# Experts with four buffers, sums by a tree, and half of the shared expert moved behind the experts

## The chip, the core and the metric

The program runs on one core of a Trainium2 chip, as a single launch. The metric is device time in microseconds (us), the median of several executions. The engines are TensorE (PE, its weight loads PEld), VectorE (DVE), ScalarE (ACT), GpSimd (POOL) and SyncE (SP), which here only issues transfers. Each engine works through its own list of instructions in order and waits on semaphores; a transfer is issued by an engine and then runs on 16 DMA engines.

## What is computed

Two transformer layers on 4096 tokens of width 256, all in float32. Layer 0 is an attention with 16 heads and linear biases, then a mixture of 64 experts; layer 1 is a rotary causal attention of one head, then a gated linear attention.

```python
x = L0_attn_x                                         # 1 x 4096 x 256
h = _layernorm(x) * (1 + ca) + sa
x = x + ga * _L0_attn_ref(h, L0_attn_W_kqv)
h = _layernorm(x) * (1 + cb) + sb
x = x + gb * _L0_ffn_ref(h, ...)                      # routed experts + shared expert
...
x = x + ga * _L1_attn_ref(h, ...)
...
x = x + gb * _L1_ffn_ref(h, ...)

# _L0_ffn_ref: 64 experts, 8 for each token, at most 256 tokens to an expert
h = silu(einsum('ech,efh->ecf', xe, w1)) * einsum('ech,efh->ecf', xe, w3)
ye = einsum('ecf,ehf->ech', h, w2)
out = segment_sum(vals * flat_w[:, None], flat_t, num_segments=T)   # the 8 rows of each token
shared = silu(x @ shared_gate.T) * (x @ shared_up.T) @ shared_down.T
return out + shared
```

## The kernel before

The residual `xres` stays in SBUF: 32 tiles of 128 tokens, in 8 chunks of 4 tiles (512 tokens). The program is a series of blocks; each ends when all engines and all its transfers are done, and only then does the next one start. The order on each engine is written out by hand. The blocks are these, with the stretch of the profiled execution (span 5162.3 us) in which each lies:

- `project_heads` (34 to 209 us): for each chunk the norm on DVE, transposes `psT`, the four blocks `psQ` of queries and keys and the values `psV` on PE. ACT copies `psQ` to `parts[b][:, 0]` (L287), DVE puts the remainder in `parts[b][:, 1]` (L327), and SP stores both parts to `q_laid` and `k_laid` (L260): 8 transfers of 256 KB a chunk. There is one buffer `parts[b]` for each block, so ACT's copy of a chunk waits for the stores of the one before. ACT copies the values to `vbuf` (L295) and issues four stores to `v_aug` itself (L300), in pieces of 512 bytes. Behind these on ACT stands the square root (L201) for which the norm of the next chunk but one waits.
- `bias_attention` (209 to 2909 us): the attention of layer 0; at its side the tokens of seven of the eight chunks are normalised (kept in `hT_rows`), routed and scattered to `x_rows`.
- `shared_expert` (2909 to 3028 us): norm and routing of the last chunk (`last_c`, 7), then `send_rows`: 32 indirect scatters by POOL (L577), each waiting for the last but one to have landed (`two_under_way`). PE does the shared expert for all eight chunks: `gate_up` (L1421, 16 products of 512 columns), ACT `Silu` (L1342), DVE `multiply` (L1364), PE `down` (L1433), DVE `add_shared` (L1370, L1374). Chunks 0 and 1 go beside the routing; 2 to 7 come after it.
- `experts` (3028 to 3318 us): a loop over 64 experts. In iteration e PE does `turn(e+2)` (transposes `psX`, L1627), `first(e+1)` (`psH`, `psU`, L1638) and `last(e)` (`psY`, L1647). DVE's `pick` takes the weights of the tokens, `multiply` makes `hidden`, and `scale` (L1601) makes `y`. SP issues four transfers an iteration: `x` of expert e+4 (320 KB) once `turn(e+2)` and `pick(e+2)` are done, `w1w3` of e+3 (256 KB), `w2` of e+2 (128 KB) and the store of `y` (256 KB). Everything has two buffers.
- `rope_attention` (3318 to 4107 us): POOL gathers eight rows of `y_rows` for each token, 8 indirect transfers a tile (L1724), into `rows[n % 2]`. DVE's `sum_rows(n)` is a reduction over 2048 elements (L1892), a product with the gate (L1895) and a sum into `xres` (L1896). At first four tiles are summed, then come `statistics(0)`, `normalise(0)` (L1921 to L1929), PE's `turn_h(0)` (L1737), `heads` with DVE's `rotate`, and tiles 4 and 5. Then runs the loop over 32 tiles of queries, where tile s holds `sum_rows(s + 6)` ahead of `maximum(s + 1)` on DVE; ACT's exponential of tile s+1 needs that maximum (`ra_top`), and PE's transposes `psT` of tile s+1 need the exponential.
- `low_rank` and `linear_attention` (4107 to 5162 us).

```python
def sum_rows(n):
    dve.wait_ge(gathered[n % 2], 16 * TOPK * (n // 2 + 1))
    dve.tensor_reduce(total[n % 2][:, :], rows[n % 2][:, :, :].rearrange("p k d -> p d k"), AX,
                      ALU.add).then_inc(rows_read, 1)
```

## Time and profile before

| | us |
|---|---|
| median of 3 runs | 5146.05 |
| lowest, highest | 5146.01, 5150.23 |
| profiled execution | 5163.93, of which the span is 5162.3 |
| PE, DVE busy in it | 4681.8 (91%), 4057.1 (79%) |
| ACT, POOL busy in it | 3071.8 (60%), 1114.2 (22%) |

The profile is of one execution, 17.9 us longer than the median of the runs. Since every block ends with a meeting of all engines, the span is the sum of its blocks, and each block has a limit of its own. What a piece of work is worth is therefore read inside its block, by which wait there ends last, and not from the shares of the whole span.

### The profile page before, as it was taken

To read this page: it belongs to the slowest core of one execution; us is meant where nothing else is said; L and a number is where in the kernel's file an instruction comes from. 1 tells how busy PE (TensorE), PEld (TensorE's weight loads), DVE (VectorE), ACT (ScalarE), POOL (GpSimd) and SP (SyncE) were. 2 spreads that over 40 slices of the span, in tenths; PEclk is the share of its full clock that TensorE was granted. 3 is DMA by queue.
4 is the path that set the end of the run, shared out by engine and by line. 5 is a ranking of instruction groups with operands and counts; after the bars stand their busy time and mean duration, and the time that the engine had idled before them with its cause. 6 is when DMAs were issued, how large, how long until landed. Compare 5 with 4: busy or idle time off the path is not lost. (4 is left out here: it accounts for less than half of the span.)

```text
span 5162.3 us, 101254 instructions
## 1 busy us (share of the span) xinstructions
PE 4681.8 (91%) x39032; PEld 2403.0 (47%) x39032; DVE 4057.1 (79%) x5031; ACT 3071.8 (60%) x5309; POOL 1114.2 (22%) x1152
## 2 busy tenths in 40 slices
PE   5589999999999999999999888547899969999998
PEld 3233333333333333333333456425566646666666
DVE  4499999999999999999998233377765448788787
ACT  1158888888888888888888512112222225555554
POOL 0000012102121021211212210254320004444443
PEclk8679999999999999999999989879999979999999
DMA  5736545354443534444342137632110031111010
GB/s 181 165 87 156 137 75 114 67 90 90 80 81 71 89 72 89 78 75 85 67 86 53 33 107 224 202 95 79 60 55 4 11 125 31 28 27 29 25 29 17
DMA packets 242778, 421.66 MB, mean 82 GB/s; under 512 B 42569, under 2 KB 147034, under 8 KB 242256
## 3 DMA queue, kind: packets, MB, share of 16 engines
q1 hardware_dynamic: 195504, 341.87, 30.1%
q0 software_dynamic: 30048, 66.76, 4.1%
q10 hardware_dynamic: 16896, 8.39, 0.7%
q8 instruction: 236, 3.87, 0.3%
q14 instruction: 94, 0.77, 0.1%
HBM read 324.51 MB, written 129.17 MB: 88 GB/s over the span
## 5 line engine op out<-in xcount | busy, mean ns | idle before, releaser
L1100 DVE TENSOR_REDUCE attn_mpart<-attn_ps_max 128x2 f32<-128x1024 f32 x2048 | 2450.0, 1221 | 100.6 <-PE attn_ps_max L1154 95.0
L837 ACT ACTIVATE attn_probs<-attn_ps_exp 128x512 f32<-128x512 f32 x4096 | 2226.7, 595 | 315.0 <-PE attn_ps_exp L1170 231.4
L1154 PE MATMUL attn_ps_max<-attn_keys,attn_quer 54*128 54x512 f32 x4096 | 1481.4, 458 | 69.9 <-DMA attn_keys<-k_laid 37.9
L1170 PE MATMUL attn_ps_exp<-attn_quer,attn_keys 54*128 54x512 f32 x4096 | 1504.2, 447 | 0.2 <-ACT attn_probs L837 0.2
L1185 PE MATMUL attn_ps_out<-attn_probs,attn_vals 128*32 128x256 f32 x16384 | 1310.1, 391 | 9.8 <-ACT route_o L842 9.2
L1170 PEld LDWEIGHTS attn_ps_exp<-attn_quer,attn_keys 54*128 54x128 f32 x4096 | 616.2, 185 | 836.2 <-ACT attn_probs L837 781.4
L1185 PEld LDWEIGHTS attn_ps_out<-attn_probs,attn_vals 128*32 128x32 f32 x16384 | 323.4, 108 | 750.3 <-issue 394.9
L1154 PEld LDWEIGHTS attn_ps_max<-attn_keys,attn_quer 54*128 54x128 f32 x4096 | 591.7, 188 | 119.3 <-DVE attn_mpart L1100 75.9
L1724 POOL DMA_INDIRECT ra_rows<-y_rows,slots x256 | 252.8, 987 | 300.8 <-DVE ra_total L1892 227.0
L577 POOL DMA_INDIRECT x_rows<-route_pay,route_now x256 | 252.0, 984 | 299.9 <-DMA x_rows<-route_pay,route_now 213.0
L1856 ACT ACTIVATE ra_row<-ra_psS 128x512 f32<-128x512 f32 x112 | 66.9, 597 | 360.9 <-PE ra_psS L1777 360.9
L1796 PE MATMUL ra_psO<-ra_vals,ra_probT 128*128 128x256 f32 x1056 | 256.5, 388 | 7.8 <-DVE ra_probT L1972 7.8
L2379 POOL TENSOR_TENSOR gla_ke<-gla_kg,emask 128x512 f32<-128x512 f32 x128 | 152.2, 1217 | 514.7 <-DVE gla_kg L2605 514.7
L1777 PE MATMUL ra_psS<-ra_kT,ra_qT 128*128 128x512 f32 (+3 forms) x576 | 240.7, 573 | 6.6 <-DVE ra_kT L1942 6.6
L1796 PEld LDWEIGHTS ra_psO<-ra_vals,ra_probT 128*128 128x128 f32 x1056 | 198.9, 196 | 42.4 <-DVE ra_probT L1972 10.0
L2670 PE MATMUL gla_psP<-gla_wqkv,gla_hc 128*128 128x512 f32 x384 | 189.7, 631 | 2.5 <-ACT gla_egn L2459 2.0
L2464 ACT ACTIVATE gla_sq<-gla_psO 128x512 f32<-128x512 f32 x32 | 19.1, 597 | 266.4 <-PE gla_psO L2778 266.4
L2365 POOL TENSOR_TENSOR gla_qeT<-gla_ftT,gla_emr 128x512 f32<-128x512 f32 x128 | 173.1, 1385 | 14.0 <-ACT gla_ftT L2411 14.0
L1777 PEld LDWEIGHTS ra_psS<-ra_kT,ra_qT 128*128 128x128 f32 x576 | 109.2, 197 | 124.8 <-issue 114.3
L1594 DVE TENSOR_TENSOR exp_hidden<-exp_psU,exp_gate 128x256 f32<-128x256 f32 x64 | 27.2, 425 | 174.0 <-PE exp_psY L1647 144.1
L1972 DVE COPY ra_probT<-ra_psT 128x512 f32<-128x512 f32 (+2 forms) x144 | 90.2, 644 | 84.6 <-PE ra_psT L1787 83.7
L1892 DVE TENSOR_REDUCE ra_total<-ra_rows 128x256 f32<-128x2048 f32 x32 | 116.9, 3653 | 39.7 <-DMA ra_rows<-y_rows,slots 39.7
(390 smaller groups left out, 5346.8 us busy)
## 6 DMA issues: line engine op xcount, KB each, us to landing
attn_keys<-k_laid SPq DMA_DIRECT2D x256, 256.0 KB
attn_vals<-v_aug SPq DMA_DIRECT2D x128, 512.0 KB, 7.7
attn_keys<-k_laid SPq DMA_DIRECT2D x256, 128.0 KB
x_rows<-attn_zeros POOLq DMA_DIRECT2D x16, 1280.0 KB, 6.2
exp_x<-x_rows SPq DMA_DIRECT2D x64, 320.0 KB
exp_w1w<-in_w SPq DMA_DIRECT2D x64, 256.0 KB
y_rows<-exp_y SPq DMA_DIRECT2D x64, 256.0 KB
attn_keys<-k_laid SPq DMA_DIRECT2D x256, 48.0 KB
```

Of the source, the lines that this page charges most:

```text
L577: pool.indirect_dma_start(out=x_rows, out_offset=bass.IndirectOffsetOnAxis(ap=r.now[:, n, k:k + 1].bitcast(U32), axis=0), in_=r.pay[:, n, ...
L837: act.activation(probs[k % 2][:, j, :], ps_exp[bank_of(g, n)][:, :], ACT.Exp).then_inc(exp_done, 1)
L1100: dve.tensor_reduce(mpart[i][:, kb, TC * pair + tile::TC * NPR], ps_max[buffer][:, :, :], AX, ALU.max).then_inc(unit_read, 1)
L1154: mm = pe.matmul(ps_max[buffer][:, h, :], quer[at % NG][half(h), pair, tile * P:(tile + 1) * P], keys[at % 2][half(h), pair, kb * CH:(kb + ...
L1170: pe.matmul(ps_exp[bank_of(g, n)][:, :], keys[g % 2][half(h), pair, k * P:(k + 1) * P], quer[g][half(h), pair, :], start=True, stop=True). ...
L1185: mm = pe.matmul(ps_out[j * VW:(j + 1) * VW, n], vals[:, k, j * VW:(j + 1) * VW], probs[k % 2][:, j, n], start=(k == 0 and q == 0), stop=( ...
L1724: pool.indirect_dma_start(out=rows[n % 2][:, k, :], out_offset=None, in_=y_rows, in_offset=bass.IndirectOffsetOnAxis(ap=slots[:, n, k:k + ...
L1777: mm = pe.matmul(psS[g % 2][:, 0:width], qT[s // TC % 2][:, k, s % TC * P:(s % TC + 1) * P], kT[:, k, b * BLK:b * BLK + width], start=(k = ...
L1796: mm = pe.matmul(psO[s % 2][:, :], probT[(before(s) + b) % 2][:, j * P:(j + 1) * P], vals[:, n, :], start=(n == 0), stop=(n == s))
L2365: last = pool.tensor_tensor(qeT[:, b, :, :], ftT[:, 3, b, :].unsqueeze(1).to_broadcast([P, NE, P]), emr[i][:, :, :], ALU.mult)
L2379: last = pool.tensor_tensor(ke[i][:, e, :], kg2[:, :], emask[:, bass.ds(m, 1), e].to_broadcast([P, KDV]), ALU.mult)
L2670: mm = pe.matmul(ps, hc[i][:, k, :], wqkv[:, x, k, :], start=(k == 0), stop=(k == KD - 1))
```

## The change

- **Projection**: `parts` gets a second set of four buffers, so that ACT's copy of a chunk waits for the stores of the chunk before the last. `vbuf` is laid out by groups of heads, so that a store goes in pieces of 2048 bytes; POOL issues one store of 1 MB a chunk in place of ACT's four; ACT copies the values in four pieces, not two.
- **Shared expert**: `shared_expert` does chunks 0, 1, 2 and 7. Its scatters wait for the last but three. Chunks 3 to 6 go to the head of `rope_attention`, beside the gathers, with weights and activations in parts of `row` that aren't in use yet.
- **Experts**: `x`, `w1w3` and `w2` get four buffers, and SP loads `x` of e+6, `w1w3` of e+5 and `w2` of e+4. `y`, `xT`, `hidden` and all of PSUM keep two. `scale` multiplies with the gate as well.
- **Sums**: `sum_rows` adds in halves (1024, 512 and 256 elements) in place of the reduction; its product with the gate is gone.

```diff
-        parts = [sb(f"parts{b}", [P, NPART, CH], F32R) for b in range(4)]
-        vbuf = [sb(f"vbuf{i}", [P, TC, H0, VW]) for i in range(2)]
+        parts = [[sb(f"parts{i}{b}", [P, NPART, CH], F32R) for b in range(4)] for i in range(2)]
+        vbuf = [sb(f"vbuf{i}", [P, NG, TC, HG * VW]) for i in range(2)]
...
+                with pool.Fori(0, NC // 2) as t:
+                    for i in range(2):
+                        hold(pool, v_copied, NG * (2 * t + i + 1), pool_passed)
+                        pool.dma_start(v_aug[:, :, bass.ds((2 * t + i) * TC, TC), :].rearrange("g p n w -> p g n w"),
+                                       vbuf[i][:, :, :, :]).then_inc(v_stored[i], 16)
...
-                        act.wait_ge(parts_stored[b], 16 * NPART * c)
+                        act.wait_ge(parts_stored[i][b], 16 * NPART * t)
...
-                    for g in range(NG):
-                        act.dma_start(v_aug[g, :, bass.ds(c * TC, TC), :],
-                                      vbuf[i][:, :, HG * g:HG * g + HG, :].rearrange("p n h w -> p n (h w)")
-                                      ).then_inc(v_stored[i], 16)
...
+SHARED_HERE = (0, 1, 2, NC - 1)
+SHARED_LATER = (3, 4, 5, 6)
...
-                    if i >= 2:
-                        pool.wait_ge(scattered[i % 2], 16 * (i // 2))
+                    if i >= 4:
+                        pool.wait_ge(scattered[i % 4], 16 * (i // 4))
...
-                for c in range(2, NC):
-                    gate_up(c)
-                    down(c - 1)
-                down(last_c)
+                for i in range(2, len(SHARED_HERE)):
+                    gate_up(i)
+                    down(i - 1)
+                down(len(SHARED_HERE) - 1)
...
+        DEEP = 4
...
-                    if more(4):
+                    if more(DEEP + 2):
...
-                        load_x(e + 4, i)
-                    if more(3):
+                        load_x(e + DEEP + 2, (i + 2) % DEEP)
+                    if more(DEEP + 1):
                         hold(sp, h_summed, e + 2, sp_passed)
-                        load_w13(e + 3, 1 - i)
-                    if more(2):
+                        load_w13(e + DEEP + 1, (i + 1) % DEEP)
+                    if more(DEEP):
                         hold(sp, y_summed, CT * (e + 1), sp_passed)
-                        load_w2(e + 2, i)
+                        load_w2(e + DEEP, i)
...
-                        dve.tensor_scalar(y[i][:, c, :], psY[i][:, c, :], wrow[i][:, c:c + 1], None,
-                                          ALU.mult).then_inc(y_copied, 1)
+                        dve.scalar_tensor_tensor(out=y[i % 2][:, c, :], in0=psY[i % 2][:, c, :],
+                                                 scalar=wrow[i % 2][:, c:c + 1], in1=mod[:, GB, :],
+                                                 op0=ALU.mult, op1=ALU.mult).then_inc(y_copied, 1)
...
+                pe.wait_ge(sw_loaded, 48)
+                gate_up(0)
+                for i in range(1, len(SHARED_LATER)):
+                    gate_up(i)
+                    down(i - 1)
+                down(len(SHARED_LATER) - 1, range(2))
                 pe.wait_ge(w_loaded, 16)
                 turn_h(0)
+                down(len(SHARED_LATER) - 1, range(2, TC))
...
-                    dve.tensor_reduce(total[n % 2][:, :], rows[n % 2][:, :, :].rearrange("p k d -> p d k"), AX,
-                                      ALU.add).then_inc(rows_read, 1)
+                    at = rows[n % 2]
+                    summing(dve.tensor_tensor(at[:, 0:4, :], at[:, 0:4, :], at[:, 4:8, :], ALU.add))
+                    summing(dve.tensor_tensor(at[:, 0:2, :], at[:, 0:2, :], at[:, 2:4, :], ALU.add))
+                    dve.tensor_tensor(total[n % 2][:, :], at[:, 0, :], at[:, 1, :], ALU.add).then_inc(rows_read, 1)
                     dve.wait_ge(rows_read, n + 1)
-                    summing(dve.tensor_tensor(total[n % 2][:, :], total[n % 2][:, :], mod_before[:, GB, :], ALU.mult))
                     summing(dve.tensor_tensor(xres[:, n, :], xres[:, n, :], total[n % 2][:, :], ALU.add))
...
                 for n in range(TC):
+                    if n < len(SHARED_LATER):
+                        multiply(n)
                     sum_rows(n)
+                    if n + 1 < len(SHARED_LATER):
+                        add_shared(n)
                 statistics(0)
                 normalise(0)
+                add_shared(len(SHARED_LATER) - 1)
```

The new `gate_up`, `down`, `multiply` and `add_shared` in `rope_attention` are those of `shared_expert` with other buffers, except that `down` and `add_shared` go tile by tile (256 columns) through the two buffers `psO`.

On ACT, in the loop of the projection, this stood from the second copy of the values to the next square root:

```order
L294 REGISTER_ALU
L295 ACTIVATE proj_vbuf<-proj_psV 128x32x16
L298 ISA
L300 ISA
L300 DMA v_aug<-proj_vbuf 128x4x128
L300 ISA
L300 DMA v_aug<-proj_vbuf 128x4x128
```

and this stands there now, the values' copies halved in size:

```order
L306 REGISTER_ALU
L308 ACTIVATE proj_vbuf<-proj_psV 128x4x4x16 x2
L306 REGISTER_ALU
L308 ACTIVATE proj_vbuf<-proj_psV 128x4x4x16 x2
L200 ISA
L201 ACTIVATE proj_rstd<-proj_rstd 128x4
```

The square root no longer stands behind four issues; the store is now alone in a loop of POOL.

On DVE, at the head of the rotary attention, this stood for the first two of the four tiles:

```order
L1892 TENSOR_REDUCE ra_total<-ra_rows 128x256
L1895 TENSOR_TENSOR ra_total<-ra_total,mod 128x256
L1896 TENSOR_TENSOR xres<-xres,ra_total 128x256
L1892 TENSOR_REDUCE ra_total<-ra_rows 128x256
L1895 TENSOR_TENSOR ra_total<-ra_total,mod 128x256
L1896 TENSOR_TENSOR xres<-xres,ra_total 128x256
```

and this stands there now for the first one (L2090 is the shared expert's `multiply`, L2096 and L2098 its `add_shared`):

```order
L2090 TENSOR_TENSOR ra_row<-ra_psT,ra_row 128x512 x2
L1973 TENSOR_TENSOR ra_rows<-ra_rows 128x1024
L1974 TENSOR_TENSOR ra_rows<-ra_rows 128x512
L1975 TENSOR_TENSOR ra_total<-ra_rows 128x256
L1977 TENSOR_TENSOR xres<-xres,ra_total 128x256
L2096 TENSOR_TENSOR ra_row<-ra_psO,mod 128x256
L2098 TENSOR_TENSOR xres<-xres,ra_row 128x256
L2096 TENSOR_TENSOR ra_row<-ra_psO,mod 128x256
L2098 TENSOR_TENSOR xres<-xres,ra_row 128x256
```

So each of the four sums stands behind a `multiply` that waits for PE and ACT, and ahead of an `add_shared` that waits for PE.

On PE, in the same place, the shared expert's products now stand around the transposes of the first chunk, `turn_h(0)` (L1784), which used to be the first in the block:

```order
L1878 MATMUL ra_psS<-ra_row 128x512 x2
L1878 MATMUL ra_psT<-ra_row 128x512 x2
L1888 MATMUL ra_psO<-ra_row 128x256 x12
L1784 MATMUL ra_psR<-ident,ra_h_head 128x128 x8
L1888 MATMUL ra_psO<-ra_row 128x256 x4
L1793 MATMUL ra_psR<-ra_hT,ra_w 128x512
```

The last half of the fourth chunk's `down` lies between the transposes and the first of the `heads`.

## Rows read from the trace of the kernel before

**Rows 1.** Window, attention block: PE, PEld, DVE, ACT, POOL busy, clock, DMA share, GB/s

```profile
209.19:2908.90 2699.71, 2643.71 (x24870) 1000.35 (x24870) 2532.70 (x2568) 2261.05 (x4185) 431.93 (x485) 0.98 0.45 86
```

**Rows 2.** Timeline of the projection: start, duration, instruction, [idle before, releaser]

```profile
100.03 0.60 ACT L287 ACTIVATE proj_parts<-proj_psQ 128x512 fp32r<-128x512 f32 x1 [7.07 <-DMA k_laid<-proj_parts]
102.74 5.65 ACTq L300 DMA_DIRECT2D v_aug<-proj_vbuf  x4
```

**Rows 3.** The same timeline, issues by SP and the end of the block

```profile
113.94 3.46 SPq L260 DMA_DIRECT2D q_laid<-proj_parts  x4
117.64 7.67 SPq L260 DMA_DIRECT2D k_laid<-proj_parts  x4
...
190.22 6.93 SPq L260 DMA_DIRECT2D k_laid<-proj_parts  x4
209.19 2.39 SPq L718 DMA_DIRECT2D attn_quer<-q_laid  x6
```

**Rows 4.** The same timeline, PE without a wait

```profile
59.44 1.04 PE L348 MATMUL proj_psT<-ident,proj_h 128*128 128x128 f32 x8
...
63.77 7.03 PE L357 MATMUL proj_psQ<-proj_hT,proj_w_kqv 128*128 128x512 f32 x16
```

**Rows 5.** DMA queues from 46 to 200 us: packets, MB, share of 16 engines

```profile
q1 hardware_dynamic: 10625, 21.50, 42.8%
q10 hardware_dynamic: 16486, 8.19, 22.3%
```

**Rows 6.** Timeline of the scatters on POOL, and SP's first issue for the experts

```profile
2949.74 0.97 POOL L577 DMA_INDIRECT x_rows<-route_pay,route_now  x1 [0.30 <-issue]
...
2999.75 0.97 POOL L577 DMA_INDIRECT x_rows<-route_pay,route_now  x1 [0.61 <-issue]
...
3028.15 0.38 SPq L1520 DMA_DIRECT2D exp_x<-x_rows  x1
```

**Rows 7.** Timeline of PE, shared expert: two chunks

```profile
2985.03 1.96 PE L1421 MATMUL disp_psG<-disp_hs,disp_wg 128*128 128x512 f32 x4 [0.88 <-DVE disp_actT L1364]
...
2996.47 1.95 PE L1421 MATMUL disp_psG<-disp_hs,disp_wg 128*128 128x512 f32 x4 [0.88 <-DVE disp_actT L1364]
```

**Rows 8.** DMA queue from 3060 to 3290 us, in the experts

```profile
q1 hardware_dynamic: 43819, 51.85, 71.2%
```

**Rows 9.** Timeline of PE in the experts: first(1), first(2), and turn(63)

```profile
3038.97 1.03 PE L1638 MATMUL exp_psH<-exp_xT,exp_w1w 128*128 128x256 f32 x4
...
3041.99 1.03 PE L1638 MATMUL exp_psH<-exp_xT,exp_w1w 128*128 128x256 f32 x4
...
3305.96 0.66 PE L1627 MATMUL exp_psX<-ident,exp_x 128*128 128x128 f32 x4 [0.64 <-DMA exp_x<-x_rows]
```

**Rows 10.** Waits of PE from 3044 to 3315 us: total, times, longest

```profile
PE exp_psX L1627 <- DMA exp_x<-x_rows: 36.4, 45, 1.9
```

**Rows 11.** Timeline of the rotary attention's head

```profile
3361.86 3.59 DVE L1892 TENSOR_REDUCE ra_total<-ra_rows 128x256 f32<-128x2048 f32 x1 [5.59 <-DMA ra_rows<-y_rows,slots]
3365.49 0.42 DVE L1895 TENSOR_TENSOR ra_total<-ra_total,mod 128x256 f32<-128x256 f32 x1
...
3373.98 1.94 PE L1737 MATMUL ra_psR<-ident,ra_h_head 128*128 128x128 f32 x8 [60.17 <-DVE ra_h_head L1929]
...
3407.95 3.59 DVE L1892 TENSOR_REDUCE ra_total<-ra_rows 128x256 f32<-128x2048 f32 x1 [3.91 <-DMA ra_rows<-y_rows,slots]
```

**Rows 12.** Timeline of DVE and POOL around 3562 us

```profile
3562.25 1.23 DVE L1925 TENSOR_TENSOR ra_scratch<-ra_scratch,mod 128x1024 f32<-128x1024 f32 x1
...
3562.40 1.89 POOL L1724 DMA_INDIRECT ra_rows<-y_rows,slots  x1 [0.30 <-issue]
```

**Rows 13.** Waits of PE from 3457 to 3920 us

```profile
PE ra_psT L1787 <- ACT ra_row L1864: 11.8, 5, 5.1
PE ra_psR L1737 <- DVE ra_h_head L1929: 11.3, 4, 4.3
PE ra_psR L1746 <- ACT ra_hT L1840: 11.1, 4, 4.9
```

## What the change will do to the time

> **What bounds the kernel now.** I read the windows by block first, since blocks never overlap, then in each block the waits of its busiest engine, and the timeline where a wait repeats. The attention is more than half of the span and none of it is touched: PE is busy 2643.7 of its 2699.7 us [rows 1]. The change touches four places, and in each the profile shows something else that ends last.
>
> In the projection it is a ring of issues. PE without waits does a chunk in 63.77 + 7.03 - 59.44 = 11.36 us [rows 4], but the last four stores of `k_laid` are issued at 190.22 and those of four chunks earlier at 117.64 [rows 3]: 18.1 us a chunk. ACT spends 5.65 us issuing the stores of the values, and has before that waited 7.07 us for a store of `parts` [rows 2]; the square root for the next norm stands behind both. After PE's last product the stores still have to be issued and to land: the issue ends at 197.15, the next block starts at 209.19 [rows 3].
>
> In `shared_expert` PE ends it. The last scatter goes out at 2999.75, SP's first load for the experts only at 3028.15 [rows 6], since PE needs 11.43 us for a chunk [rows 7] and six are still ahead of it when routing is done.
>
> In `experts` the loads end each iteration. `turn` goes from 3038.97 (its end, for e=2) to 3305.96 (e=63) in 61 steps: 4.38 us each, where two early iterations, whose data were there, took 3.02 [rows 9]. PE waits for `x` 36.4 us in 45 times [rows 10], while the DMA engines are 71.2% busy [rows 8]: neither is at its limit, so it is the distance between an issue and its use.
>
> At the head of `rope_attention` the gathers end last: PE is idle for 60.17 us, DVE waits 5.59 us for the rows of the fourth tile [rows 11]. Later PE is the bound with short waits for DVE and ACT [rows 13].
>
> **Projection, -49 us.** *Issues:* the four of ACT go to POOL (5.65 us off ACT a chunk), and the wait for `k_laid` goes with the second set of `parts`. SP's four stores take 3.46 us beside nothing and 7.67 beside ACT's [rows 3]; one issue of POOL in place of four by ACT should leave most at 3.46, 7 us a chunk, under PE's 11.36. So PE is late next. Its product Q(1) starts at 63.77, Q(7) at 63.77 + 6 x 11.36 = 131.9 and ends at 139; the stores behind it are out by 139 + 2 x 3.46 = 146; with the landing of before (209.19 - 197.15 = 12.0) the next block starts at 158, and I take 160 for a clock or a buffer that comes late. *Transfers:* queues 1 and 10 hold the engines 42.8% + 22.3% of 154 us, 100.3 us of all 16 [rows 5]. Queue 10, the values, takes 34.3 us for 8.19 MB, 4.19 us a MB; queue 1, in larger pieces, 3.07. Values in pieces of 2048 bytes at queue 1's price save 9.2 and leave 91. From some 55 on this would end at 146 on engines always busy, hidden under PE; at the 71.2% that the experts reach [rows 8] it ends at 183. Ends: -26 and -54 (no landing beyond 7 us). I take -49, nearer to PE's rows, because the queues hold whole chunks of work at once.
>
> **Shared expert, -34 us.** Four chunks off PE: its end goes from 3027.3 (0.9 before SP's first load) to 3027.3 - 4 x 11.43 = 2981.6, and then the scatters are last. Thirty-one are spread from 2949.74 to 2999.75, 1.67 us each; without a wait one takes 0.97 and 0.30 between [rows 6], so the last goes out at 2949.74 + 30 x 1.28 = 2988.1. With its 0.97, some 2.3 for landing and 0.9 for the meeting of the engines SP starts at 2992 to 2994 if four under way never wait, at 2997 if they wait half of what they do now. Gain 31 to 36; I take 34. Here PE is hidden by some 10 us; without that cover a chunk more would have cost 11.43.
>
> **Experts, -60 us.** The loads are issued four experts ahead of use, not two, and the latency goes. Next is the larger of three. PE: 3.02 [rows 9]. DMA: 51.85 MB at 71.2% of 230 us are 163.8 us of all engines [rows 8]; an expert moves 983,040 bytes, so 3.11 us. SP: four issues, between 0.38 each [rows 6] and 3.46 / 4 = 0.87 [rows 3], so 1.5 to 3.5. A loop never keeps all three full: I take 3.4. 61 x (4.38 - 3.4) = 60. Ends: 61 x (4.38 - 3.11) = 77, and 30 for 3.9 (the first rival). The three transfers issued before the loop become more (for four experts), which the first `turn` waits for by one issue at most, 1 us. `scale` now also multiplies by the gate; a product of the same 256 columns with two tensors takes 0.42 us [rows 11], about what the scaling alone does, and DVE isn't last: nothing.
>
> **Rope attention's head, +10 us.** The removed chunks come back here. Let T be 3318.05, the block's start. The gathers are ready for the fourth sum at T + 43.8, it ends at T + 47.4, and PE has `h_head` at 3373.98, T + 55.9 [rows 11]. After it each sum stands behind a `multiply`. A chunk is 11.43 us of PE, ACT and DVE [rows 7]; with one sum in between I take 12.5. The first starts at about T + 8, when its weights are in, and its products are half a step late because PE comes cold: m3 is ready at 8 + 3 x 12.5 + 9 = 54.5, the sum with its 2.9 and the wait at 58.5; from the sum to PE's transposes it takes 3373.98 - 3366.3 = 7.7 as before: T + 66.2, so +10.3 us. It isn't given back: the next tile's sum, at 3407.95, waits for gathers too [rows 11], and these wait for the buffer that the fourth sum frees. Half a `down` behind `turn_h(0)` costs PE 2 us, beside ACT's copy. Ends: 0 (the gathers' own pace stays last) and +21 (`gate_up` twice as slow, next rival).
>
> **Sums, -22 us.** The reduction takes 3.59 and the two products 0.42 each: 4.6 with gaps. Now: 1024 columns 1.23 [rows 12], 512 about 0.69, a bound from between 0.42 (256) and 1.23; two of 256 at 0.42 [rows 11]; with gaps 2.9. It saves 1.7 us a tile. Only where PE waits behind DVE does this count. From 3457 to 3920 the three largest such waits are 11.8, 11.3 and 11.1 us in 13 times [rows 13], most longer than 1.7, and nearly every one has a sum ahead of it: 13 x 1.7 = 22. Ends: 0, and 26 x 1.7 = 44 if every later sum were on the path. A rule speaks against this edit. A gather beside a two-input sum over 1024 columns took 1.89 us where it otherwise takes about 0.95 [rows 12], and there was no such thing beside the reductions. The Trainium skill ("SBUF — State Buffer", Who interferes with whom) says that a DVE instruction with two SBUF inputs contends with a GpSimd instruction that reads SBUF, and that `tensor_reduce` never does. By it the three sums of a tile would hold up the gathers; by the first rows alone they would cost nothing there. I keep it as a rival, below.
>
> Another rule touches the projection. The row has 3.46 us for SP's four issues alone and 7.67 beside ACT's. The Trainium skill ("DMA: Bandwidth & Descriptors", Issuing engines are not separate DMA queues) says that issuing from several engines saves only the sequencer's time, usually small. By that rule alone the gain would be ACT's 5.65 us in each of seven chunks, 40 us; the sum above has 49.
>
> **Sum.** -49 - 34 - 60 + 10 - 22 = -155: the profiled 5163.93 becomes 5009. The median of the runs was 17.9 lower than that execution, so 4991. Attention, `low_rank` and linear attention: nothing.
>
> **Rivals.**
> 1. *The store of `y` keeps the experts.* `y` still has two buffers, and its store now stands in the queue behind loads for four experts. If `scale` waits for it, an iteration stays near 3.9: -30 in place of -60, 5021. For: same queue, engines at 71.2%. Against: in PE's waits of before no such wait leads; `x` does [rows 10]. 12%.
> 2. *Slow clock in the head.* PE idles for long there, so the four chunks may run at 1.2 GHz: 10.5 us more each, +42 if all four, about 5033. For: PE's idle 60 us. Against: it now works from T + 8. 8%.
> 3. *Sums hold up the gathers.* A tile's eight gathers at 1.89, not 0.95, would be 15 us, still under a loop step except at the head and where PE already waits; it takes the 22 back: 5013. 8%.
> 4. *Transfers bound the projection.* -26 instead of -49: 5014. 10%.
> 5. *Slower than before: attention clock.* Attention needs 2643.7 us of PE at 0.98 of full clock [rows 1]. If another entry into it left PE at 1.2 GHz for a stretch of 155 us of work, it would be 310 us long and all is lost: 5146 and above. From there it decides. For: 0.98 means that some 100 us were slow already. Against: PE is 98% busy and the granted clock rose. 2%.
>
> My own case has 60%, with 4970 to 5012 from the ends of experts and projection. With rivals 1 to 4 the range that holds 8 in 10 is 4955 to 5035. Faster than before by over 0.2% (10 us, about what a measurement of this kernel can tell from no change): 97%; within it 1%; slower 2%.
>
> **What the profile of after would show.** Projection: right if the next block starts near 209 - 49 and ACT no longer waits for `k_laid`; wrong if SP's issues stay over 5 us or POOL's store waits. Shared expert: SP's first load 34 earlier relative to the block's start, scatters 1.28 apart, PE done before. Experts: 3.4 us between two `turn`s, `x` gone from PE's waits; a wait of DVE for `y`'s store shows rival 1. Head: `turn_h(0)` 66 us after the block's start, the first `gate_up` at +8 with its clock. Sums: 2.9 us a tile, gathers at 0.95. The prediction is wrong as a whole if two of experts, projection and sums give half.

## The result, and the profile after

The changed kernel takes 5061.47 us (median of 4 runs, 5051.75 to 5066.8), the kernel before 5146.03; the ratio is 0.9834, with a 95% interval of 0.9817 to 0.9852. It is faster by 85 us where 155 were forecast, and 5061 lies above the range of 4955 to 5035. Timed again later (label after_again, below) the ratio was 0.9817.

These are the windows by block of the changed kernel. The columns are the length, busy time of PE, PEld, DVE, ACT and POOL, PE's granted clock, DMA share and GB/s. The blocks are, row by row, attention, shared expert, experts, rotary attention, the two blocks at the end together, and the projection.

```profile
193.31:2896.00 2702.69, 2645.57 (x24870) 1001.16 (x24870) 2532.51 (x2568) 2260.60 (x4185) 431.88 (x485) 0.98 0.45 86
2896.00:2980.18 84.18, 52.51 (x170) 30.36 (x170) 41.23 (x108) 9.99 (x14) 33.06 (x35) 0.84 0.10 31
2980.18:3221.34 241.16, 209.84 (x1024) 168.78 (x1024) 93.86 (x256) 62.81 (x128) 0.00 (x0) 0.98 0.83 261
3221.34:3999.95 778.61, 669.55 (x2608) 439.67 (x2608) 464.88 (x904) 185.17 (x240) 256.66 (x258) 0.95 0.20 59
3999.95:5065.20 1065.25, 969.05 (x10016) 683.31 (x10016) 793.32 (x1057) 513.32 (x667) 390.06 (x363) 0.94 0.13 39
34.00:193.31 159.31, 100.16 (x320) 58.56 (x320) 69.13 (x160) 38.64 (x89) 9.59 (x12) 0.80 0.64 209
```

Each block but the projection is counted from SP's first transfer of it, which gives the same limits in every run. The projection is counted from 33.9 us in all of them; its first transfer goes out at 32.7 to 34.0. The terms of the prediction stand beside what they came to, in this profile and in that of the same kernel profiled a second time:

| block | before | forecast | after | difference | second profile |
|---|---|---|---|---|---|
| projection | 175.3 | -49 | 159.4 | -15.9 | -22.8 |
| attention | 2699.7 | 0 | 2702.7 | +3.0 | -0.7 |
| shared expert | 119.2 | -34 | 84.2 | -35.1 | -33.0 |
| experts | 289.9 | -60 | 241.2 | -48.7 | -48.5 |
| rotary attention | 790.9 | -12 | 778.6 | -12.3 | -8.8 |
| the last two blocks | 1053.3 | 0 | 1065.3 | +11.9 | +8.7 |
| span | 5162.3 | -155 | 5065.2 | -97.1 | -105.2 |

Two terms were too large, the projection by 33 and the experts by 11; nothing forecast the 15 us that two unchanged blocks gave away.

A block also varies by itself, and the differences below have to be read beside that. The changed kernel's projection took 152.5 to 162.4 us in the eight profiles that keep it, and its rotary attention 775.0 to 782.1 in the eight that keep that. The experts of the kernel before took 289.9 us here and 279.9 in the run sixteen_before, which doesn't touch them.

**Projection.** First the timeline of ACT, then that of SP, in the changed kernel: start, duration, instruction, and in brackets the wait before it.

```profile
92.69 0.60 ACT L299 ACTIVATE proj_parts<-proj_psQ 128x512 fp32r<-128x512 f32 x1 [2.63 <-DMA k_laid<-proj_parts]
99.71 0.60 ACT L299 ACTIVATE proj_parts<-proj_psQ 128x512 fp32r<-128x512 f32 x1 [6.42 <-DMA k_laid<-proj_parts]
```

```profile
94.40 7.15 SPq L263 DMA_DIRECT2D k_laid<-proj_parts  x4
101.92 6.89 SPq L263 DMA_DIRECT2D q_laid<-proj_parts  x4
109.12 10.29 SPq L263 DMA_DIRECT2D k_laid<-proj_parts  x4
...
173.44 10.23 SPq L263 DMA_DIRECT2D k_laid<-proj_parts  x4
193.31 2.40 SPq L727 DMA_DIRECT2D attn_quer<-q_laid  x6
```

The wait for `k_laid` of [rows 2] is still there, in every chunk from the fourth on, though a chunk now waits for the stores of the last but one. SP's four issues, forecast at 3.46 as in the first line of [rows 3], take 5 to 10 us from then on, and ACT issues nothing any more. PE shows the same. These are its products of the third to the sixth chunk:

```profile
74.28 7.03 PE L364 MATMUL proj_psQ<-proj_hT,proj_w_kqv 128*128 128x512 f32 x16
...
85.47 7.03 PE L364 MATMUL proj_psQ<-proj_hT,proj_w_kqv 128*128 128x512 f32 x16
...
101.41 9.26 PE L364 MATMUL proj_psQ<-proj_hT,proj_w_kqv 128*128 128x512 f32 x16 [4.58 <-ACT proj_hT L292]
...
118.37 8.83 PE L364 MATMUL proj_psQ<-proj_hT,proj_w_kqv 128*128 128x512 f32 x16 [3.37 <-ACT proj_hT L292]
```

Chunks are 11.2 us apart until both sets of `parts` are full, close to the 11.36 of the forecast, and 15 to 17 from then on. So the second set of buffers put off the start of the jam to the fourth chunk, and the jam stayed.

**Shared expert.** The timeline of the end of the block, of PE, DVE, POOL and SP:

```profile
2960.28 3.69 PE L1443 MATMUL disp_psA<-disp_wd,disp_actT 128*128 128x256 f32 x16 [2.07 <-DVE disp_part L1380]
```

```profile
2964.73 0.69 DVE L1384 TENSOR_TENSOR xres<-xres,disp_part 128x512 f32<-128x512 f32 x1
```

```profile
2935.53 0.97 POOL L584 DMA_INDIRECT x_rows<-route_pay,route_now  x1 [0.31 <-issue]
...
2974.24 0.98 POOL L584 DMA_INDIRECT x_rows<-route_pay,route_now  x1 [0.30 <-issue]
```

```profile
2980.18 0.37 SPq L1538 DMA_DIRECT2D exp_x<-x_rows  x1
```

The scatters are 1.29 us apart on the mean ((2974.24 - 2935.53) / 30) and last; PE and DVE were done at 2965.4, 9.8 us before the last scatter ended. Both as forecast.

**Experts.** DVE's and PE's first rows of waits from 2990 to 3221 us (total, times, longest), each the first of its answer; `x` is nearly gone from PE's.

```profile
DVE exp_y L1621 <- DMA y_rows<-exp_y: 107.1, 52, 3.1
```

```profile
PE exp_psY L1672 <- DVE exp_hidden L1614: 20.4, 28, 1.1
...
PE exp_psX L1652 <- DMA exp_x<-x_rows: 0.2, 1, 0.2
```

**Rotary attention.** The first product of the shared expert on PE, its last one ahead of `turn_h(0)`, and `turn_h(0)`:

```profile
3229.35 3.45 PE L1878 MATMUL ra_psS<-ra_row 128*128 128x512 f32 x4 [12.29 <-DMA ra_row<-in_w_down]
...
3277.66 1.99 PE L1888 MATMUL ra_psO<-ra_row 128*128 128x256 f32 x8 [2.48 <-DVE ra_row L2090]
3287.73 1.94 PE L1784 MATMUL ra_psR<-ident,ra_h_head 128*128 128x128 f32 x8 [8.08 <-issue]
```

They stand at 8.0, 56.3 and 66.4 us after the block's start. Forecast were 8, then 54.5 for the last `multiply`, for which that product waits, and 66.2. The slow clock of rival 2 showed only in the first four products of the first chunk and of the third, 3.45 and 3.58 us where the others take 1.88; the granted clock was 0.93, 1.00 and 0.88 over the stretches of the first three chunks.

### The profile page after: what moved, and what is told of

The parts are those of the page before. It is cut to its first block and busy times, and to the rows that moved or that the text cites. A ratio compares the mean times of both kernels' runs of the same rounds, so it can differ in the third digit from the quotient of the medians.

```text
span 5065.2 us, 100979 instructions
## 1 busy us (share of the span) xinstructions
PE 4659.7 (92%) x39032; PEld 2387.3 (47%) x39032; DVE 4006.8 (79%) x5079; ACT 3072.6 (61%) x5325; POOL 1122.8 (22%) x1160
## 5 line engine op out<-in xcount | busy, mean ns | idle before, releaser
L1109 DVE TENSOR_REDUCE attn_mpart<-attn_ps_max 128x2 f32<-128x1024 f32 x2048 | 2448.9, 1220 | 111.5 <-PE attn_ps_max L1163 105.2
L1843 PEld LDWEIGHTS ra_psO<-ra_vals,ra_probT 128*128 128x128 f32 x1056 | 196.1, 193 | 36.1 <-issue 7.5
L1621 DVE SCALAR_TENSOR_TENSOR exp_y<-exp_psY,exp_wrow,mod 128x256 f32<-128x256 f32 x128 | 56.0, 479 | 114.1 <-DMA y_rows<-exp_y 107.1
L2879 PE MATMUL gla_psO<-gla_s_mid,gla_qeT 128*128 128x128 f32 x1024 | 135.3, 275 | 0.0
```

What stands on the lines that cost most here:

```text
L1109: dve.tensor_reduce(mpart[i][:, kb, TC * pair + tile::TC * NPR], ps_max[buffer][:, :, :], AX, ALU.max).then_inc(unit_read, 1)
L1843: mm = pe.matmul(psO[s % 2][:, :], probT[(before(s) + b) % 2][:, j * P:(j + 1) * P], vals[:, n, :], start=(n == 0), stop=(n == s))
L2879: mm = pe.matmul(o, queries, s_mid[:, b, e, :, :].rearrange("p h d -> p (h d)"), start=False, stop=(b == NPAIR - 1 and e == NE), skip_grou ...
```

## The experiments

All were made from the changed kernel unless they say otherwise. Block lengths are those between SP's first transfers, as in the table above; only the blocks that an edit touches are named. v_twice, near_loads and two_scatters were executed once each, so for them there is a profile and no interval.

### What bounds the projection

The theory of the prediction was a ring of issues (B); its rival was the transfers (A). In k_by_pool the stores of `k_laid` change the engine that issues them:

```diff
-                        for b in range(NB):
+                        for b in range(2):
...
+                        for b in range(2, NB):
+                            hold(pool, qk_parts, NB * (c + 1) + b + 1, pool_passed)
...
+                                pool.dma_start(rows, parts[i][b][:, part, :].bitcast(F32)).then_inc(parts_stored[i][b], 16)
```

> The changed kernel, but the stores of k_laid are issued by POOL and only those of q_laid by SP. In the changed kernel PE did its first three chunks of the projection in 11.2 us each and later ones in 15 to 17; ACT waited 39.5 us for k_laid, and the block took until 193.3. Theory A (the transfers bound the projection: 2 MB on SP's queue and 1 MB on POOL's in about 15.5 us a chunk): the chunks stay at 15 to 16 us and the block ends within 5 us of 193. Theory B (one engine's row of eight issues, each waiting for the parts of its own block, bounds it): the chunks fall to 11.2 and the block ends 25 to 35 us earlier, as predicted.

The projection took 160.1 us, against 159.4, and the kernel 5058.78: nothing. ACT now waited for `q_laid` instead, 55.7 us in 8 times.

In v_twice each chunk's values are stored twice:

```diff
+                        pool.dma_start(v_again[:, :, bass.ds((2 * t + i) * TC, TC), :].rearrange("g p n w -> p g n w"),
+                                       vbuf[i][:, :, :, :]).then_inc(v_stored[i], 16)
```

> The changed kernel, but POOL stores the values of each chunk twice, the second time to a spare tensor that nothing reads. Queue 0 had 8.39 MB for 20.3% of 142 us, 28.8 us of all engines. Theory A (transfers bound the projection): the block gets 29 us longer if the engines fill up, up to 44 us at the share of 0.65 that they had. Theory B (issues bound it): POOL is idle, so 0 to 5 us.

196.1 us, 36.7 more for 8.39 MB (34 to 44 over the eight profiles of the unchanged projection). So the transfers bound the block, and theory B falls. But these are the DMA shares in 40 equal slices of the changed kernel's window from 95 to 175 us, as tenths, and what its two queues held (packets, MB, share of 16 engines):

```profile
DMA  4455488544445795545557964455498455555985
...
q1 hardware_dynamic: 5322, 10.26, 37.7%
q0 software_dynamic: 1340, 5.17, 22.6%
```

A resource that bounds the work should be full, and this one stands at 0.4 to 0.5 for whole stretches, and above that only where values are stored too. The stores of queries and keys write rows of 8 heads by 16 dimensions, the head outermost. So the next theory (C) was that such a store runs on 8 of the 16 engines. The edit puts the dimensions outermost in `parts`, by the order of the weights' columns:

```diff
-                                sp.dma_start(rows, parts[i][b][:, part, :].bitcast(F32)).then_inc(parts_stored[i][b], 16)
+                                sp.dma_start(rows.rearrange("h d n -> d h n"),
+                                             parts[i][b][:, part, :].bitcast(F32)).then_inc(parts_stored[i][b], 16)
...
+                    act.activation(w_turned[:, k, :].rearrange("p (b d h) -> p b d h", d=HD0, b=NB),
+                                   w[:, k, 0:2 * D].rearrange("p (b h d) -> p b d h", d=HD0, b=NB),
+                                   ACT.Copy).then_inc(w_set, 1)
```

> The changed kernel, but the rows of queries and keys lie in parts by dimension and then head, not by head and then dimension (ACT copies the weights once in that order before the first norm, 2 x 512 columns), so that each store of 256 KB has 16 rows outermost in memory instead of 8. Same bytes, same pieces of 2 KB, same number of issues. The DMA engines were only 0.4 to 0.5 busy in the stretches without a store of values and 0.9 with one, though a backlog stood in the queue. Theory C (a store whose outermost dimension is 8 runs on 8 of the 16 DMA engines): a store goes twice as fast, the chunks fall to about 11.2 us and the block ends 25 to 35 us earlier. Theory D (all 16 are used and the writes themselves are slow): no change, within 3 us.

The projection took 113.9 us, 45.5 less and so more than expected, and the kernel 5013.08 (ratio to the kernel before 0.9725, 0.9702 to 0.9747). The same view for it, from 95 to 145 us, then ACT's waits from 46 to 148:

```profile
DMA  9999922999999944999999914999999999889999
...
q1 hardware_dynamic: 5281, 9.61, 60.2%
q0 software_dynamic: 1321, 5.15, 27.2%
```

```profile
ACT proj_parts L301 <- PE proj_psQ L372: 37.8, 32, 3.9
ACT proj_vbuf L310 <- PE proj_psV L381: 16.8, 16, 1.2
```

The shares are at nine tenths in most slices, and ACT waits for PE, for no store. Its chunks are 11.2 us apart to the end:

```profile
117.99 7.03 PE L372 MATMUL proj_psQ<-proj_hT,proj_w_turned 128*128 128x512 f32 x16
...
129.19 7.03 PE L372 MATMUL proj_psQ<-proj_hT,proj_w_turned 128*128 128x512 f32 x16
```

That a store went twice as fast with the same bytes and pieces is measured; that it is 8 engines against 16 is inferred, since the view does not tell the engines apart. The shares of 0.4 to 0.5 point to it, and so does the time that the packets of queue 1 held the engines: 37.7% of 80 us for 10.26 MB before the edit, 60.2% of 50 us for 9.61 MB after it, which is 2.9 and 3.1 us of all 16 for a MB. The packets got no faster; more of them were under way at a time. So a transfer does not always run on all 16 engines, as the first section has it. The Trainium skill ("DMA: Bandwidth & Descriptors", Why a DMA increments its semaphore by 16 and not by 1) says that a transfer runs on the largest number of engines up to 16 that divides the outermost sizes of both of its sides; these runs agree.

Last the same edit in the kernel before, without anything else of the change:

> The kernel before with one change alone: 16 rows outermost in the stores of queries and keys. Theory A (the slow stores were the root of the block's time in the kernel before too, and its waits for k_laid and much of ACT's 5.65 us of issuing were their backlog): the projection goes from 175.3 to 115 to 130 us, and the second set of parts and the moved issue are worth little beside it. Theory B (ACT's issues and the single parts bound the kernel before by themselves): at most 15 us.

The projection took 139.7 us, 35.6 less than 175.3, and the kernel 5125.36 (ratio 0.9949, 0.9934 to 0.9965). It lies between the two expectations. The edit alone is worth about twice what the whole change gave this block (13 to 23 us over the profiles). The rest, 139.7 to 113.9, is what the change's own edits there are worth together once the stores are fast: the second `parts`, POOL's issue, and the values in larger pieces and four copies, which were not tried one by one. ACT had waited 34.5 us for `k_laid` in the kernel before, from 46 to 200 us, and 2.9 are left. Its other wait, time in which it issued the stores of the values, goes from 38.1 us only to this (46 to 150 us):

```profile
ACT proj_rstd L201 <- issue: 25.9, 6, 5.3
```

| projection, us | stores with 8 outermost | stores with 16 outermost |
|---|---|---|
| kernel before | 175.3 | 139.7 |
| changed kernel | 159.4 | 113.9 |

### What bounds the experts

In y_four, `y` has four buffers as the loads do:

```diff
-        y = [sb(f"y{i}", [P, CT, D]) for i in range(2)]
+        y = [sb(f"y{i}", [P, CT, D]) for i in range(DEEP)]
...
-                    dve.wait_ge(y_stored[i % 2], 16 * (DEEP // 2 * t + i // 2))
+                    dve.wait_ge(y_stored[i], 16 * t)
```

> The changed kernel with four buffers of y too. DVE waited 107.1 us in 52 times for the store of y, and an expert took about 3.65 us. Theory A (the store of y, queued behind the deep loads, held the loop, rival 1 of the prediction): 3.2 to 3.35 us an expert, the experts 18 to 25 us shorter. Theory B (the DMA engines, 84.7% busy, are at their practical limit): 3.55 to 3.65 and at most 5 us; DVE's wait is then slack.

The experts took 205.9 us, 35.3 less and so more than theory A expected: rival 1 was at work in the changed kernel, though an expert took 3.63 there and not the 3.9 that it was priced at. The kernel took 5022.21 (ratio 0.9729, 0.9702 to 0.9757), on the same chip as the 5058.78 of k_by_pool. One window in the middle of the loop, of y_four and then of the changed kernel:

```profile
3000.00:3180.00 180.00, 180.00 (x951) 158.69 (x950) 86.73 (x239) 57.90 (x118) 0.00 (x0) 1.00 0.97 319
```

```profile
3000.00:3200.00 200.00, 178.69 (x881) 143.27 (x881) 80.42 (x220) 53.93 (x111) 0.00 (x0) 1.00 0.86 267
```

An expert has 16 products in these counts, so y_four takes 180 / (951 / 16) = 3.03 us for one, with PE never idle, and the changed kernel 3.63. The DMA engines reach 0.97: the 0.86 was no limit either.

In near_loads, `y` keeps its four buffers and the loads go out as late as in the kernel before:

```diff
-                        load_x(e + DEEP + 2, (i + 2) % DEEP)
+                        load_x(e + 4, i)
...
-                        load_w13(e + DEEP + 1, (i + 1) % DEEP)
+                        load_w13(e + 3, (i + 3) % DEEP)
...
-                        load_w2(e + DEEP, i)
+                        load_w2(e + 2, (i + 2) % DEEP)
```

> The changed kernel with four buffers of y, but with the loads of the experts issued as late as before (x of e+4, w1w3 of e+3, w2 of e+2). Theory A (both the distance of the loads and the buffers of y are needed): about 4.2 to 4.4 us an expert, the experts' block 275 to 290 us. Theory B (y's two buffers were the only limit, also in the kernel before): about 3.1 us and 206 us. What PE waits for tells them apart too: x by A, nothing by B.

283.8 us, 4.30 for an expert from 3000 to 3240, as theory A has it. PE's waits from 3000 to 3250 us:

```profile
PE exp_psX L1652 <- DMA exp_x<-x_rows: 31.5, 49, 2.0
PE exp_psH L1663 <- DMA exp_w1w<-in_w: 9.1, 30, 1.5
```

The block is 6 us shorter than the 289.9 of the kernel before, but 4 longer than the 279.9 of the same code in sixteen_before, and what differs most is the clock. It stood at 0.81 in the first 62 us of the block here and in the first profile, and at 0.84 in the first 42 in sixteen_before. These are stretches at full clock, of near_loads, sixteen_before and the kernel before:

```profile
3042.00:3242.00 200.00, 165.69 (x765) 124.83 (x765) 69.71 (x192) 47.11 (x96) 0.00 (x0) 1.00 0.74 235
3034.00:3254.00 220.00, 183.12 (x845) 138.19 (x846) 74.85 (x210) 51.63 (x105) 0.00 (x0) 1.00 0.75 236
3210.00:3310.00 100.00, 83.22 (x384) 62.69 (x383) 34.63 (x97) 23.55 (x48) 0.00 (x0) 1.00 0.73 233
```

They make 4.18, 4.17 and 4.17 us for an expert (another stretch of the kernel before, 3090 to 3190, makes 4.28). So with late loads four buffers of `y` are worth nothing that can be told from the scatter. Early loads with two buffers of `y` gave 39 to 49 us, by which profile of the late loads one takes, and both together 74 to 84.

### Shared expert and rotary attention

In all_here all eight chunks come before the experts (`SHARED_HERE` has all of them, the rest is left out of the rotary block):

> The changed kernel with all eight chunks of the shared expert before the experts, none beside the gathers. Theory A (the terms of the prediction): the shared block 34 to 37 us longer, the rotary block 9 to 12 us shorter, in sum 24 us slower than the changed kernel. Theory B (the head of the rotary block hid the chunks wholly): 35 us slower.

Shared expert 116.9 us, 32.7 longer; rotary attention 766.6, 12.0 shorter. In sum the blocks are 20.7 longer, and the median is 5082.94 (ratio 0.9866, 0.9836 to 0.9895). The move is worth what its two terms said, within 4 us. The same run measures the sums: its rotary block is that of the kernel before with the three sums and without the product, and it is 24.3 us shorter than the 790.9 there.

Five_here has one chunk more before the experts and three beside the gathers:

```diff
-SHARED_HERE = (0, 1, 2, NC - 1)
-SHARED_LATER = (3, 4, 5, 6)
+SHARED_HERE = (0, 1, 2, 3, NC - 1)
+SHARED_LATER = (4, 5, 6)
```

> The changed kernel with chunk 3 of the shared expert back before the experts, so five there and three beside the gathers. In the changed kernel PE and DVE were done there at 2965.4 and the last scatter ended at 2975.2, a cover of 9.8 us; a chunk is 11.4. In the head of the rotary block the chain over the chunks took 12.6 us for each. Theory A (scatters last before the experts, chunks last in the head): 0 to 2 us more in the shared block, 10 to 12 us less in the rotary block. Theory B (the gathers were about as late as the chunks): at most 3 us less.

83.8 and 768.3 us: 10.7 less in sum, by theory A, and 5049.07 for the kernel (ratio 0.9798, 0.9774 to 0.9822). The 10.3 in the rotary block alone are 7 to 14 against the other profiles. `turn_h(0)` came 55.1 us after the block's start, about where it was before the change [rows 11]. The cover of 9.8 us took in a chunk of 11.4 for nothing to be seen.

Two_scatters has the scatters two under way again:

```diff
-                    if i >= 4:
-                        pool.wait_ge(scattered[i % 4], 16 * (i // 4))
+                    if i >= 2:
+                        pool.wait_ge(scattered[(i - 2) % 4], 16 * ((i - 2) // 4 + 1))
```

> The changed kernel with the scatters of the shared block two under way again instead of four. Theory A (scatters end the block, six waits of 9.7 us in all before): 7 to 11 us longer there. Theory B (the norm and routing ahead, or PE, end it): 0 to 2 us.

89.2 us, 5.0 more than in the first profile and 3.0 more than in the second: the right sign, less than theory A expected. The scatters are 1.47 us apart, where four under way gave 1.29 and the kernel before had 1.67. POOL waited for a scatter once, 1.0 us, and was idle for up to 0.7 us between the others, against 0.3 with four; the long waits of up to 2.7 us of the kernel before did not come back. The chunks of the shared expert that SP loaded beside them are gone in this kernel. The run all_here has these loads back, with four under way, and its scatters are 1.28 us apart. So beside the loads four under way took away all of the waits, and without the loads two under way cost only half as much.

In reduce_again the reduction takes the place of the three sums:

```diff
-                    summing(dve.tensor_tensor(at[:, 0:4, :], at[:, 0:4, :], at[:, 4:8, :], ALU.add))
-                    summing(dve.tensor_tensor(at[:, 0:2, :], at[:, 0:2, :], at[:, 2:4, :], ALU.add))
-                    dve.tensor_tensor(total[n % 2][:, :], at[:, 0, :], at[:, 1, :], ALU.add).then_inc(rows_read, 1)
+                    dve.tensor_reduce(total[n % 2][:, :], rows[n % 2][:, :, :].rearrange("p k d -> p d k"), AX,
+                                      ALU.add).then_inc(rows_read, 1)
```

> The changed kernel with the reduction over 2048 elements back in place of the three sums (the product with the gate stays gone). Theory A (the sums are worth the predicted 22 us, less the 0.42 us a tile that the missing product gives by itself, so about 1.3 of 1.7): the rotary block gets 15 to 19 us longer. Theory B (the 22 came from elsewhere and the sums are off the path): 0 to 5 us. Theory C (two-input sums hold up the gathers): a gather takes 0.95 us beside reductions and the block gets shorter, not longer.

The rotary block took 794.2 us, 15.6 more than in the first profile; over the runs with the three sums and the same head (775.0 to 782.1) it is 12 to 19. The kernel took 5075.28 (ratio 0.9834, 0.9809 to 0.9859), 16.5 more than k_by_pool on the same chip. The gathers in the changed kernel, then in this one (count, busy time, mean ns of one, idle time before):

```profile
L1771 POOL DMA_INDIRECT ra_rows<-y_rows,slots x256 | 254.9, 996 | 285.0 <-DVE ra_total L1975 210.3 <-issue 74.7
```

```profile
L1771 POOL DMA_INDIRECT ra_rows<-y_rows,slots x256 | 251.3, 982 | 305.5 <-DVE ra_total L1972 232.1 <-issue 73.3
```

14 ns a gather, 3.6 us in all, on an engine that waits 210 us for DVE in that block: rival 3 is too small to matter. Single gathers do get longer: 24 of the 256 took over 1.1 us in the changed kernel (15 in the kernel before), each beside a product or sum of two tensors on DVE, while no gather without one beside it took more than 1.02.

### All repairs together, and the changed kernel again

> The changed kernel with all three repairs: sixteen rows outermost in the stores of queries and keys, four buffers of y, and chunk 3 of the shared expert back before the experts. The blocks are separate, so the gains should add: 45.6 in the projection, 35.3 in the experts, 10.3 in the rotary block and 0.4 before it, 92 us off the changed kernel's 5061, so 4966 to 4975 by the theory that each repair took away a wait of its own. The rival (the DMA engines, 97% busy with four buffers of y, or clock, give some of it back elsewhere): 4985 or more.

4973.76 us (median of 5 runs, 4958.54 to 4974.52), ratio to the kernel before 0.9643 (0.963 to 0.9656). The experts took 205.5 us, the projection 114.2, the rotary block 769.0, each about as alone. The attention, without an edit, took 2706.9, 4 us more than in any other profile. The time lies within what was expected, and below both kernels'.

> The changed kernel unchanged, timed again against the kernel before on one chip. By blocks the two profiled executions differ by 97.1 us, the medians first measured by 84.6. Theory A (the blocks are right, and the 12 us are which executions were profiled and on which chip): a difference of 90 to 100 us, with the blocks of projection, shared expert, experts and rotary attention within 4 us of the first profile. Theory B (the profile of the kernel before was a slow one, its blocks too long by 12 us somewhere): 82 to 88 us.

5058.68 us against 5156.5 on the same chip, a difference of 97.8; the ratio 0.9817 (0.9801 to 0.9832) is 94 us with 87 to 103 as its interval. So theory A, but not in all of it: the projection took 152.5 us, 6.9 less than in the first profile, beyond the 4 us that were expected. The kernel before had medians of 5146, 5162, 5155, 5152 and 5156 in the five comparisons, so a part of the missing 12 us is on which chip and in which execution one looks. Another part is in the profile of the kernel before, as theory B had it: its experts took 10.0 us more than the same code in sixteen_before, with a lower clock for longer.

## Why the prediction was wrong, step by step

The distance from 4991 to 5061.5 is 70.5 us. Of it 33.1 are the projection, 11.3 the experts, 14.9 the unchanged blocks, and 12.6 that the profiled execution of the kernel before lay 17.9 above its median and that of the changed kernel only 5.3; shared expert and rotary block take 1.4 off. The prediction called itself wrong as a whole if two of experts, projection and sums gave only half. Only the projection did, with a third, and it alone is nearly half of the distance.

- **Projection: the step that failed is the reading of 7.67 us as ACT's issues in SP's way.** A row of four issues contains the wait for the parts of the next block between them. The runs show it: ACT issues nothing in the changed kernel and the rows grow to 10 us, while with 16 rows outermost they take 2.6 to 3.2, but for one of 4.3. So the wait for `k_laid` was not mainly a matter of issues and buffers: the stores themselves were slow, which neither a second set of `parts` nor another issuer changes. Rival 4 (transfers bound the projection) came true, and beyond its -26: -16 and -23 were measured. The part on PE was right (11.2 us a chunk). Once the stores were fast the block took 113.9 where 126 were forecast, since the last stores were out sooner (140 for 146) and landed in 7.6 us, not the 12.0 taken from before. Right was also the work of the DMA engines: 91 us forecast, 64.6% of the 142 us from 46 to 188 measured, 91.7. What failed there was the share at which they could be used. The end of my range took 0.712 from the experts, whose transfers have other shapes; the block's own rows showed less, 0.65 [rows 5]. This is the same view of the kernel before, 95 to 190 us, with the fours and fives that I did not ask about:

```profile
DMA  4455986125588763456968545569860355877644
```

- **The rule on issuing engines** of the Trainium skill ("DMA: Bandwidth & Descriptors", Issuing engines are not separate DMA queues), weighed against the 49 us: by it the gain would have been 40, still far above 16. Neither the forecast nor that estimate asked how fast a store was. The run k_by_pool, where the issues were shared between two engines for no gain (160.1 us for 159.4), agrees with the rule itself.
- **Shared expert: right** in mechanism and size (-35 and -33 for -34), scatter spacing and cover included. The spacing fell from 1.67 to 1.28 us in all_here too, which loads beside the scatters what the kernel before did, so the fall is that of four under way.
- **Experts: right mechanism, wrong next bound.** The step that failed is the choice of the next bound among three. PE at 3.02, DMA at 3.11 and SP were compared, and 3.4 taken because "a loop never keeps all three full". But y_four keeps PE (3.03) and the DMA engines (0.97) full together. What held the changed kernel was none of the three, but a round trip. These are DVE's `scale`, the store of its `y`, and the next `scale` into the same buffer, which in the timeline is the next but one:

```profile
3099.57 0.87 DVE L1621 SCALAR_TENSOR_TENSOR exp_y<-exp_psY,exp_wrow,mod 128x256 f32<-128x256 f32 x2 [2.21 <-DMA y_rows<-exp_y]
...
3107.46 0.88 DVE L1621 SCALAR_TENSOR_TENSOR exp_y<-exp_psY,exp_wrow,mod 128x256 f32<-128x256 f32 x2 [1.52 <-DMA y_rows<-exp_y]
```

```profile
3102.95 0.41 SPq L1557 DMA_DIRECT2D y_rows<-exp_y  x1
```

From the end of the first at 3100.44 the store waits 2.5 us behind SP's loads, is away for 4.5, and the next takes 0.9: 7.9 us for two experts here, 7.3 on the mean. Its parts, the order of SP's issues and the landing of a store, were there to be priced before. The argument against rival 1, that no such wait stood in the profile of before, was empty: near_loads shows that with late loads the loads come first, whatever the buffers of `y`. Whether the store placed ahead of SP's loads would have done as well as four buffers was not tried. Besides, the 4.38 us an expert from which the forecast started held stretches of low clock. At full clock it was 4.17 to 4.28, so some 6 to 13 us of the forecast, 61 times the difference, were not the latency of the loads.
- **Head of the rotary block: right**, 66.4 for 66.2. By all_here the head cost 12 us, 8 to 16 over the profiles, where 10 were forecast. **Sums: right in size.** By the same run they and the missing product are worth 24 us, where 22 were forecast and the block varies by 7. reduce_again puts the three sums at 12 to 19 of it, of which 15 to 19 were expected; the product was not tried by itself. That the gain comes from 13 waits of PE, as the forecast counted, no run shows.
- **Unchanged blocks: nothing was set aside for them.** The linear attention and what stands before it took 11.9 and 8.7 us more. Its first stretch in the kernel before, the changed kernel, and the second profile, some 80 us from the block's start:

```profile
4216.38:4290.00 73.62, 50.47 (x409) 29.38 (x410) 41.55 (x51) 34.21 (x40) 22.72 (x26) 0.81 0.23 70
```

```profile
4108.41:4190.00 81.59, 58.47 (x419) 32.41 (x421) 41.93 (x52) 35.76 (x42) 23.02 (x27) 0.74 0.21 64
```

```profile
4103.55:4185.00 81.45, 60.03 (x498) 34.93 (x499) 45.08 (x54) 38.89 (x46) 23.04 (x27) 0.78 0.23 70
```

The mean clock is 0.81 in the first and 0.74 in the second, with 8 us more for about as many products. In windows of 10 us the clock is at 1.00, PE's upper level (2.4 GHz), from 30 us after the block's start in the first and stays there for the next 100. In the other two it does so only from 60 us. In the third 498 products fit into the same time as the second's 419, so the way there differs between two executions of one kernel. Over all runs the linear attention took 942 to 957 us, with no edit in it. But the two profiles of kernels with the old rotary block are the two shortest (945.9 and 942.1; the twelve others 946.8 to 956.8, 951.1 on the mean), so some 7 us may come with the change after all. That was not tested, and the cause is open.

## What to carry to other kernels

Before a wait for a transfer is taken away by a buffer or another issuer, look at the share of the DMA engines while that transfer runs alone. Here they stood half full beside a backlog, and the shape of the transfer, not its place, was the matter: 16 rows outermost in place of 8 repaired it for 36 to 46 us. When loads go deeper, price the round trip of every buffer that stays at two (wait of the store behind the new loads, landing, and the work on it, over two iterations); a wait that does not appear before may only be hidden by the one that you remove. A mean step taken over a whole block should be checked for stretches of low clock before it is called latency. And a term read from a row of several issues needs the row taken apart first, since it holds the waits between them.

## What the runs showed of the hardware that was not expected

- The same 256 KB in pieces of 2 KB, with 16 rows outermost in place of 8: the DMA share rose from 0.60 to 0.87 of the window (37.7% and 22.6%, against 60.2% and 27.2%) and the throughput from 193 to 295 GB/s.
- The DMA engines kept a share of 0.97 and 319 GB/s for 180 us beside a PE that was busy all of that time.
- PE's clock reached its upper level, and kept it for at least 100 us, 30 us after the linear attention's start in one profile and 60 us after it in two others; between the first two profiles that went with 8 us.
- The same experts' code took 289.9 and 279.9 us in two executions, with the clock at 0.81 over the first 62 us of the block and at 0.84 over the first 42; at full clock both reach 4.17 us an expert.
